# Turning the softmax maxima with one transpose into sixteen short lines, in a four-layer kernel on one core

## The reference

```
x = x + _L0_xattn_ref(_layernorm(x), ctx_768, ...)      # cosine attention
x = x + _L0_ffn_ref(_layernorm(x), ...)                 # quantised FFN with a convolution
x = x + _L1_xattn_ref(_layernorm(x), ctx_768, ...)      # softmax attention, 16 heads of 32
x = x + _L1_ffn_ref(_layernorm(x), ...)                 # channel mix
```

```
q = x @ w_q + b_q ; k = context @ w_k + b_k ; v = context @ w_v + b_v     # split into 16 heads of 32
scores = jnp.einsum('bqhd,bkhd->bhqk', q, k) * scale
weights = jax.nn.softmax(scores, axis=-1)
out = jnp.einsum('bhqk,bkhd->bqhd', weights, v).reshape(B, Lq, D) @ w_o + b_o
```

## Time and profile before

| | us |
|---|---|
| median of 3 runs | 1723.47 (1720.33 to 1724.28) |
| the profiled execution: time of the run | 1720.95 |
| its span in the trace | 1718.7 |
| softmax attention in the trace, about | 643 to 1428 |
| a middle batch of it, from turning to turning (1131.21 to 1225.56) | 94.35 |
| PE busy in the span | 92% |

### The profile page before, as it was taken

How to read it: one execution, slowest core, us unless ns; L and a number is a source line. 1 busy time by engine, 2 the same in 40 slices (tenths; PEclk the granted TensorE clock), 3 DMA queues, 4 the chain that set the end, 5 groups by cost and what they waited for, 6 DMA issues and landing times. The chain is left out here.

```text
span 1718.7 us, 29488 instructions
## 1 busy us (share of the span) xinstructions
PE 1586.6 (92%) x8932; PEld 719.5 (42%) x8932; DVE 1227.2 (71%) x1756; ACT 1138.3 (66%) x1895; POOL 1023.1 (60%) x738
## 2 busy tenths in 40 slices
PE   5999878998999977999999999999999988999998
PEld 3545433444444432334444444444444423444443
DVE  4978898997989745676676767676767766655553
ACT  5667599787888734665657666665657567556662
POOL 4777436666677723565657666675756665545452
PEclk9989999999999997999999999999999989999999
DMA  8410000000000112121211212121201110010001
GB/s 309 149 70 36 1 1 1 1 1 1 0 1 1 62 48 76 32 58 26 58 34 36 57 26 57 28 55 30 59 24 40 40 44 25 25 43 30 24 24 50
DMA packets 60463, 72.22 MB, mean 42 GB/s; under 512 B 14416, under 2 KB 40016, under 8 KB 59856
## 3 DMA queue, kind: packets, MB, share of 16 engines
q1 hardware_dynamic: 56944, 62.22, 12.3%
q10 hardware_dynamic: 3424, 8.91, 1.3%
HBM read 37.40 MB, written 8.39 MB: 27 GB/s over the span
## 5 line engine op out<-in xcount | busy, mean ns | idle before, releaser
L1556 DVE TENSOR_REDUCE s_mx<-bank 128x1 f32<-128x512 f32 x512 | 336.8, 684 | 198.5 <-PE bank L1684 192.5
L1443 ACT ACTIVATE s_E<-bank 128x512 f32<-128x512 f32 x512 | 293.7, 595 | 198.7 <-PE bank L1698 173.4
L1342 POOL TENSOR_TENSOR s_E<-s_E 128x1024 f32<-128x1024 f32 x128 | 300.5, 2367 | 122.0 <-PE bank L1706 114.5
L1684 PE MATMUL bank<-s_KA,s_QA 96*128 96x512 f16 x512 | 193.2, 388 | 17.3 <-DMA s_KA<-sm_cx 7.9
L1698 PE MATMUL bank<-s_QA,s_KA 97*128 97x512 f16 x512 | 195.7, 384 | 3.3 <-DMA s_QA<-s_mrow 1.1
L1335 POOL TENSOR_TENSOR sm_cx<-s_qkf,sm_cx 128x512 f16<-128x512 f32 x64 | 76.4, 1194 | 175.9 <-ACT sm_cx L1421 175.7
L1867 POOL TENSOR_TENSOR sm_cx<-m_xf,sm_cx 128x512 f16<-128x512 f32 x60 | 84.1, 1407 | 105.7 <-ACT sm_cx L1909 105.7
L1706 PE MATMUL bank<-s_E,s_V 128*32 128x512 f32 x1024 | 136.5, 605 | 4.3 <-ACT s_E L1443 4.3
L1075 PE MATMUL bank<-sm_zz,w1raw 128*128 128x512 f16 x256 | 99.4, 388 | 30.7 <-DVE sm_cx L962 15.5
L1098 PE MATMUL bank<-f_w2q,w2raw 128*128 128x512 f16 x512 | 121.8, 379 | 0.6 <-DVE w2raw L950 0.3
L772 POOL TENSOR_TENSOR sm_wkv<-sm_wkv,sm_cx 128x511 f32<-128x511 f32 x48 | 66.1, 1378 | 92.5 <-DVE sm_wkv L962 83.0
(11 more groups left out here) (264 smaller groups left out, 4078.6 us busy)
## 6 DMA issues: line engine op xcount, KB each, us to landing
sm_cx<-in_ctx SPq DMA_DIRECT2D x16, 768.0 KB, 4.5
s_QA<-sm_cx SPq DMA_DIRECT2D x384, 32.0 KB, 1.9
s_KA<-sm_cx SPq DMA_DIRECT2D x372, 32.0 KB, 1.9
X<-in_x SPq DMA_DIRECT2D x8, 1024.0 KB, 6.9
out_x<-X SPq DMA_DIRECT2D x8, 1024.0 KB, 4.3
w1raw<-in_w ACTq DMA_DIRECT2D x1, 4096.0 KB, 14.6
w2raw<-in_w ACTq DMA_DIRECT2D x1, 4096.0 KB, 28.2
w1raw<-in_wq SPq DMA_DIRECT2D x1, 1024.0 KB, 5.4
```

The costliest lines, as they stand in the source:

```text
L1342: e.tensor_tensor(into, into, other, ALU.add).then_inc(s_sum.sem, 1)
L1443: e.activation(E[:, SLOT[k] + h, :], SC[u % 2][:, :], ACT.Exp, scale=1.0 / float(np.sqrt(DH)))\
L1556: e.tensor_reduce(mx[:, q, h:h + 1], MX[q % 2][:, :], AX.X, ALU.max).then_inc(s_red.sem, 1)
L1684: e.matmul(MX[k % 2][:, :], QA[0:MROW, m, h, q * P:(q + 1) * P], KA[0:MROW, m, h, :], start=True, stop=True).then_inc(s_mx.sem, 1)
```

## The change

The columns of `mx` are laid head by head, so that the sixteen of them are one block of 16 columns. One transpose turns them into 16 lines of 128 in place of four transposes into 4 lines of 512. ACT copies 16 lines of 128 instead of 4 of 512, and the DMA takes 16 lines of 256 bytes instead of 4 of 1024. What lies in `QA` at the end is the same.

```diff
-        mx, mrow = sb("mx", [P, TT, 4]), sb("mrow", [4, S], F16)
+        mx, mrow = sb("mx", [P, 4, TT]), sb("mrow", [4 * TT, P], F16)
...
             def rows(b, m):
                 s_mT.wait(e, b, m + 1)
                 s_md[(m - 1) % NG].wait(e, b, 1 if m else 0)
-                e.activation(mrow[:, :], MX[0][0:4, :], ACT.Copy, scale=-1.0 / MS).then_inc(s_mrow.sem, 1)
+                e.activation(mrow[:, :], MX[0][0:4 * TT, 0:P], ACT.Copy, scale=-1.0 / MS).then_inc(s_mrow.sem, 1)
                 e.wait_ge(s_mrow.sem, s_mrow.count(b, m + 1))
                 s_sc.wait(e, b, 16 * (m + 1) - 16 * NG)
-                e.dma_start(QA[MROW:MROW + 1, m, :, :], mrow[0:4, :]).then_inc(s_md[m].sem, 16)
+                e.dma_start(QA[MROW:MROW + 1, m, :, :].rearrange("o h (q n) -> o (h q) n", n=P), mrow[:, :]).then_inc(s_md[m].sem, 16)
...
-                e.tensor_reduce(mx[:, q, h:h + 1], MX[q % 2][:, :], AX.X, ALU.max).then_inc(s_red.sem, 1)
+                e.tensor_reduce(mx[:, h, q:q + 1], MX[q % 2][:, :], AX.X, ALU.max).then_inc(s_red.sem, 1)
...
             def rows(b, m):
                 e.wait_ge(s_red.sem, s_red.count(b, 16 * (m + 1)))
-                for q in range(TT):
-                    last = e.transpose(MX[0][0:4, q * P:(q + 1) * P], mx[:, q, :], ident[:, :])
-                last.then_inc(s_mT.sem, 1)
+                e.transpose(MX[0][0:4 * TT, 0:P], mx[:, :, :].rearrange("p h q -> p (h q)"), ident[:, :]).then_inc(s_mT.sem, 1)
```

## The result

| | before | changed |
|---|---|---|
| first comparison, 13 runs each | 1722.5 | 1714.87 (1705.82 to 1718.73) |
| second, 35 and 12 runs | 1717.47 | 1714.14 |
| third, 23 and 12 runs | 1716.43 | 1716.49 |
| profiled execution, its span | 1720.95, 1718.7 | 1716.18, 1713.9 |

The ratios are 0.9959 (0.9939 to 0.9979), 0.9982 (0.9965 to 0.9999) and 0.9988 (0.9971 to 1.0006). Their mean is 0.9976, or 4.1 us. The kernel before had a median of 1722.5 in the first comparison and of 1716.4 to 1718.0 in the three later ones, so the 7.6 us between the medians of the first are more than the change is worth. The third interval takes in 1, so by itself it shows no gain. The traces are much more exact than these medians, so most of what follows is read there.

A forecast was written before the change was run, and what follows sets the result against it. PE's stream was taken to bound softmax attention, except where PE waits for KA's landing. Fifteen turnings gave -4.9 us, a deduction +0.5, so 1723.47 - 4.4 = 1719.1 us, range 1713.5 to 1723.0.

The forecast's parts named there:

- the forecast's own case: Whole kernel: 1719.1 us, with 1717 to 1721; chance 0.43.
- the first rival: All turnings count, because PE does not wait for KA's landing at 1115.00: 9.9 us, about 1713.5; chance 0.15.
- The step of 0.11 us, three of them a turning: On PE at each turning, three of four transposes go, at 0.11 us each: 0.33 us saved.
- The bound of 0.17: If a 16-line transpose cost PE the whole 272 ns, a turning would save only 0.17 us.
- ACT's copy and issue gain, and that is worth nothing: On ACT, 0.63 us gained per turning, all under PE's other work, worth nothing but more to spare.
- Half of the turnings count: Per batch, savings at m = 0 and 1 count; those at m = 2 and 3 are lost waiting for KA.
- the 0.31 us at 1115.00: Idle ahead of PE's first `maximum` on KA, taken as a wait for its DMA landing.
- The chain's length: POOL, then SP's 24 DMAs, 26 us past two turnings: landed at 1114.5, PE's first `maximum` loads at 1115.00.
- Fifteen turnings, 4.9 us: 14 turnings in seven batches, plus m = 2 of the last batch: 15 x 0.33 = 4.9 us.
- 0.5 us for the keys of m = 2: Deduction: PE comes 0.65 earlier with some 0.3 to spare; at worst 2.4 us over seven batches, 0.5 taken.
- The last batch: PE waits 2.06 us for its row of maxima, late behind the w_k load, which also comes 0.33 earlier.
- Slower by short pieces: Row DMA's 256-byte pieces hold up KA's landing: a further 1.9 us each gives +8.9 us, about 1732; chance 0.08.

## Why the prediction was right

The forecast was 1723.47 - 4.4; the mean of the three ratios makes it 4.1 us, and the first comparison's 1714.87 lies in the range of 1713.5 to 1723.0. It lies outside the 1717 to 1721 of the forecast's own case and nearer to the first rival's 1713.5; what tells them apart is the batch length, 0.64 us shorter and not 1.3.

- **The step of 0.11 us, three of them a turning.** Right. The score follows 0.11 us behind the transpose. From one turning's last reduce to the next, over batches 1 to 6, the distance from m = 0 to m = 1 went from 21.09 to 20.77, and from m = 2 to m = 3 from 24.14 to 23.82: 0.32 each. The bound of 0.17 fell. The Trainium skill ("Part 4: PE-mode transpose" in TensorE: Matmul & The Clock Gate) has about 275 ns for a transpose, and the trace agrees with that for one by itself (277); the 12 us worked out from it did not come, since the next instruction follows at 0.11.
- **ACT's copy and issue gain, and that is worth nothing.** Right in that it gains nothing: the copy takes 0.27 us where I forecast 0.29, and the whole gain goes with PE's transposes alone. The issue takes 0.51, where I had left it at 0.6. What I put at nothing is a small loss: the row, issued earlier, falls just ahead of an issue of SP, and with the copy at its old length the batch is 0.12 us shorter.
- **Half of the turnings count.** Right in size, with a wrong reading in it and some luck. I took the 0.31 us at 1115.00 for a stall of PE. It is idle time of the weight load, and the product behind it started without any; the first rival said as much, and concluded that nothing was waited for. The chain's length, worked out to 1114.5 against 1115.00, says that PE had 0.5 us to spare, so by my own figures only 0.15 of the 0.65 us would have been lost. Two things that I didn't have took the rest. From the end of SP's last issue I had 1.3 us to the landing, and where PE really waits its product starts 1.56 to 1.62 behind that end, which leaves 0.2 of the 0.5. And in four of the five later batches the change made the chain 0.24 us longer, which takes the 0.2. The stall arose with the change. The distance from m = 3 to the next m = 0 grew from 20.28 to 20.53, although 0.33 us were saved in it.
- **Fifteen turnings, 4.9 us.** Between turnings of batches 1 and 7, 567.51 us became 563.81, or 0.62 a batch where I had 0.65. In the last batch, from the last reduce for m = 0 to that for m = 3, 70.47 us became 69.52: 0.95 for three turnings, so the one for m = 2 counts there, as forecast.
- **0.5 us for the keys of m = 2.** Right in size by luck, as it comes in one batch and not in seven. Behind the first batch, PE stands for them only in batch 1, 0.42 us. At the place of the earlier trace rows the load has some idle time and the product none. The changed kernel's timeline of PE, and then of its loads:

```profile
774.55 0.60 PE L1684 MATMUL bank<-s_KA,s_QA 96*128 96x512 f16 x2 [0.42 <-issue]
```

```profile
1150.09 0.15 PEld L1684 LDWEIGHTS bank<-s_KA,s_QA 96*128 96x128 f16 x2 [0.28 <-issue]
```

- **The last batch.** As forecast, the row of maxima still lands late, issued behind the load of w_k, and PE waits the same 2.06 us as in the earlier trace rows. Issuing the row 0.63 us earlier didn't get it ahead:

```profile
1369.96 0.10 PEld L1696 LDWEIGHTS bank<-s_QA,s_KA 97*128 97x128 f16 x1 [2.06 <-DMA s_QA<-s_mrow]
```

- **Slower by short pieces.** It didn't happen by way of the landing, though the row's earlier issue does hold up `KA`, by 0.24 us and not by 1.9. ACT's queue has 4192 packets instead of 3424, 24 more a turning, and in the changed kernel's view of DMA issues both kinds land in time:

```profile
s_KA<-sm_cx SPq DMA_DIRECT2D x372, 32.0 KB, 1.9
...
s_QA<-s_mrow ACTq DMA_DIRECT2D x32, 4.0 KB, 1.7
```

`KA`'s median is still 1.9 us. The row's 1.7 us to landing, on 256-byte pieces, are far inside its slack of over 4 us. The Trainium skill's rule on pieces under 512 bytes (DMA: Bandwidth & Descriptors, "Specifications"), that they are read and modified before they are written, shows no cost here. Whether a piece is slower by itself, no run of this case measures.

Still open is the part of the time that varies outside the batches. The profiled spans differ by 4.8 us, of which 3.7 lie between batches 1 and 7. The first batch's turnings, which I had as lost, can't be told apart from the 3 us by which the three profiles of the changed kernel differ there. Ahead of the first turning the changed profile is 2.5 us shorter, and behind the last 2.7 longer, in code that is the same in both.

## What to carry to other kernels

Where a repeated loop holds a chain on other engines that starts ahead of several edits and ends behind them, a saving inside it is worth only what the chain leaves, so compare its end with the arrival of the engine that waits, to a tenth of a microsecond, and not with whether that engine waits now. Then look in the changed profile whether the chain kept its length in every round, as work that comes earlier on another queue can stretch it. Put the saved work back in one part of the loop at a time: equal numbers of dummies that cost 0.04 us in one place and 0.65 in another show where the cover lies. And once a saving has run into such a chain, shorten the chain: here a wait moved behind the transfers that didn't need it, no engine's work changed, and 0.64 us a batch became 1.29.

## What was not expected of the hardware

- A transpose of f32 columns into sixteen lines adds no more to PE's stream than one into four: 0.11 us in both, 277 against 272 ns alone.
- An issue of 16 lines of 256 bytes on ACT's queue took 0.51 us, one of 4 lines of a kilobyte 0.59.
- An issue on SP's queue that starts 0.06 to 0.13 us behind the end of ACT's issue of the row took 0.79 to 0.89 us instead of 0.59, in all 41 such places of the 13 profiles but one, where it took 1.5. In the 32 places where SP's issue starts between 0.10 us before that end and 0.05 us behind it, it took 0.60 or less. What the two queues share, no run shows.
- Four times the lines made ACT's copy no slower: 267 ns for 16x128 and 0.59 us for 16x512, against 0.59 for 4x512. The columns set its time.
- The idle time of a weight load isn't PE's: 0.31 us ahead of the load went with no gap at the product.
